# A fused attention-and-experts kernel: hand-written queue orders changed on all five engines, and four turn banks instead of two for the last tile

## The reference

```
q(v)  = (clip(round(v / s + z), 0, 255) - z) * s
x = x + tanh(g_x) * matmul(q1(layernorm(x)), q2(ctx))
y = layernorm(x)
logits = y @ route_w.T                     # the best of 8 experts per row
wh = onehot(argmax) * max(logits) * (y @ A.T)
x = x + tanh(g_f) * (wh @ B.T)
```

## Time and profile before

| what | us |
|---|---|
| median of three executions (lowest, highest) | 364.46 (363.89, 364.64) |
| the profiled execution | 363.53 |
| its span, first to last instruction | 361.7 |
| PE busy | 333.0 (92%) |
| DVE busy | 260.6 (72%) |
| ACT busy | 197.4 (55%) |
| POOL busy | 172.3 (48%) |

### The profile page before, as it was taken

The page is one execution under the profiler, slowest core; times in us unless marked ns, Lnnn a source line. Parts: engine busy times, 40 slices in busy tenths (PEclk is TensorE's granted clock), DMA queues, the critical chain, the costliest instruction groups (busy, mean ns, idle before and its releaser), DMA issues.

```text
span 361.7 us, 5854 instructions
## 1 busy us (share of the span) xinstructions
PE 333.0 (92%) x2237; PEld 186.4 (52%) x2262; DVE 260.6 (72%) x553; ACT 197.4 (55%) x129; POOL 172.3 (48%) x199
## 2 busy tenths in 40 slices
PE   0389999999999999999998999999999999999983
PEld 0244454546756466455464546464464555465751
DVE  3855799898967896958658587945588567585853
ACT  1888489778967262747999270524062413204460
POOL 2559267431265162545999056627064441605281
PEclk9999999999999999999999999999999999999999
DMA  7999999895769998899799996666939890443956
GB/s 301 400 387 404 366 387 380 289 348 173 284 182 212 289 251 291 270 266 294 176 366 157 262 320 121 181 111 177 212 138 158 225 288 31 93 84 59 304 220 232
DMA packets 93906, 87.63 MB, mean 242 GB/s; under 512 B 71844, under 2 KB 72868, under 8 KB 89764
## 3 DMA queue, kind: packets, MB, share of 16 engines
q1 hardware_dynamic: 93856, 87.11, 79.5%
q10 hardware_dynamic: 12, 0.00, 0.0%
HBM read 52.49 MB, written 16.78 MB: 191 GB/s over the span
## 4 chain that ended last, share of the span: by engine, by line
PE 77%; DVE 8%; DMA 7%; issue 2%; ACT 2%; POOL 2%; ACTq 0%; SPq 0%; DVEq 0%
PE main L1575 46%; DMA xs<-in_x 4%; PE hp L1613 4%; PE hp L1617 4%; PE hp L1614 4%; PE outp L1575 4%; PE outp L1658 4%; PE outp L1660 3%; PE outp L1659 3%; DVE bn L971 3%; PE turn L1609 2%; DMA prow<-in_g_ffn 2%; DMA out<-xs 1%; ACT x L753 1%; PE turn L1503 1%
## 5 line engine op out<-in xcount | busy, mean ns | idle before, releaser
L1575 PE MATMUL main<-q,qa 128*128 128x512 bf16 x841 | 194.6, 380 | 5.0 <-POOL q L593 2.3
L1575 PEld LDWEIGHTS main<-q,qa 128*128 128x128 bf16 x864 | 83.2, 98 | 101.2 <-issue 2.7
L586 POOL TENSOR_TENSOR yn<-y,yn 128x2048 f16<-128x2048 f32 x13 | 53.0, 4077 | 31.7 <-ACT y L788 31.7
L735 ACT ACTIVATE c<-stage,zpc,inv 128x2048 int8<-128x2048 f32 x24 | 49.9, 2086 | 7.7 <-DMA stage<-in_ctx 4.0
L593 POOL CAST q<-c 128x2048 bf16<-128x2048 int8 x24 | 45.1, 1893 | 15.3 <-ACT c L735 14.8
L782 ACT ACTIVATE yn<-xs,sc 128x2048 f16<-128x2048 f32 x11 | 23.0, 2093 | 53.4 <-POOL sc L579 49.6
L1104 DVE SCALAR_TENSOR_TENSOR xs<-main,cc,xs 128x512 f32<-128x512 f32 x45 | 33.3, 740 | 21.7 <-PE main L1575 21.5
L574 POOL TENSOR_SCALAR ve<-mv 128x1 f32<-128x1 f32 x16 | 3.1, 191 | 84.8 <-DVE mv L1137 81.8
L1184 DVE SCALAR_TENSOR_TENSOR xs<-outp,tsc,xs 128x512 f32<-128x512 f32 x44 | 31.2, 735 | 13.6 <-PE outp L1660 13.5
L971 DVE BATCH_NORM_STATS2 bn<-xs 128x6 f32<-128x512 f32 x52 | 32.1, 680 | 10.6 <-DMA xs<-in_x 10.6
L753 ACT ACTIVATE x<-xs,sc 128x2048 int8<-128x2048 f32 x12 | 25.0, 2087 | 24.5 <-POOL sc L566 24.4
(11 more groups left out here) (132 smaller groups left out, 435.2 us busy)
## 6 DMA issues: line engine op xcount, KB each, us to landing
stage<-in_ctx SPq DMA_DIRECT2D x24, 1024.0 KB, 7.9
xs<-in_x SPq DMA_DIRECT2D x13, 1024.0 KB, 6.5
out<-xs SPq DMA_DIRECT2D x12, 1024.0 KB, 5.0
yT<-in_ctx SPq DMA_DIRECT2D x4, 1024.0 KB, 9.2
y<-in_ctx SPq DMA_DIRECT2D x4, 1024.0 KB, 10.1
c<-in_x SPq DMA_DIRECT2D x3, 1024.0 KB, 7.4
out<-c SPq DMA_DIRECT2D x3, 1024.0 KB, 7.3
c<-in_L_ffn_A SPq DMA_DIRECT2D x1, 1024.0 KB, 11.5
```

Of the source, the lines that this page charges most:

```text
L586: pool.tensor_tensor(yn[:, 1, :], y[:, :], yn[:, 0, :], ALU.subtract).then_inc(s_ylo_made, 1)
L735: act.activation(c8_of(piece), place(piece), ACT.Identity, bias=zpc[:, 1:2], scale=inv[:, 1:2])\
L1575: last = pe.matmul(bank_of(n)[:, :], q1T(t)[:, k, :], q2[:, nb, k, :], start=(k == 0), stop=(k == KC - 1))
```

## The change

All lists of calls are reordered, with no call added or removed; nearly every tile is touched. One mechanism is new: groups 2 and 3 of tile 15's second transposition go to the two main banks, `y_bank(15, 2)` = `mainp[1]` and `y_bank(15, 3)` = `mainp[0]`, and wait until the last two half blocks have been read.

```diff
+        def y_bank(t, g):
+
+            return mainp[3 - g] if t == T - 1 and g >= 2 else turn[g % 2]
...
+                elif t < T - 1:
+                    pe.wait_ge(s_y_split, 4 * YT.index(t) + g - 1)
                 else:
-                    pe.wait_ge(s_y_split, 4 * YT.index(t) + g - 1)
+
+                    pe.wait_ge(s_half_added, 1)
+                    pe.wait_ge(s_main_added, UNIT[T - 1, NB - 1] + 1)
```

```diff
 (PE, tiles 0 to 3, last block)
-            turn_b(0)
-            turn_b(1)
             column_sums(0, [3])
             main(0, 3, 0)
             main(0, 3, 1)
+            turn_b(0)
+            turn_b(1)
+            main(0, 3, 2)
             turn_b(2)
-            turn_b(3)
-            main(0, 3, 2)
             main(0, 3, 3)
             column_sums(1, [3])
             main(1, 3, 0)
+            turn_b(3)
...
+            turn_q1(4, 0)
+            turn_q1(4, 1)
             column_sums(2, [3])
             main(2, 3, 0)
             main(2, 3, 1)
             main(2, 3, 2)
-            spread_scales()
-            turn_q1(4, 0)
-            turn_q1(4, 1)
+            main(2, 3, 3)
             turn_y(0, 0)
             turn_y(0, 1)
-            main(2, 3, 3)
-            h_group(0, 0)
+            spread_scales()
```

```diff
 (DVE, same place)
             add_main(0, 3)
             stats2_sum(0)
             unit_terms(1, 3)
+            take_b(3)
+            scale_b()
+            take_q1T(4, 0)
+            take_q1T(4, 1)
             add_main(1, 3)
 (SP, batch change)
             load_ctx(30)
+            load_ctx(31)
             load_x(9)
-            load_ctx(31)
 (DVE, tile 8)
             add_experts(5, 0)
+            add_experts(5, 1)
             stats1(9)
             tile_terms(8)
             add_main(8, 0)
             add_main(8, 1)
-            add_experts(5, 1)
```

```diff
 (PE, the end)
+            expert_product(12, 1)
             main(15, 2, 2)
+            main_half(0, 0)
             main(15, 2, 3)
-            main_half(0, 0)
+            expert_product(12, 2)
             main_half(0, 1)
             main_half(1, 0)
             main_half(1, 1)
-            expert_product(12, 1)
-            expert_product(12, 2)
             h_rows_high(14)
             expert_product(12, 3)
             turn_wh(13)
             h_rows_low(14)
+            turn_y(15, 0)
+            turn_y(15, 1)
+            turn_y(15, 2)
             expert_product(13, 0)
             expert_product(13, 1)
-            turn_y(15, 0)
+            turn_y(15, 3)
...
             expert_product(14, 0)
             expert_product(14, 1)
+            expert_product(14, 2)
             h_group(15, 2)
             h_group(15, 3)
-            expert_product(14, 2)
             expert_product(14, 3)
 (DVE, the end)
             add_main(14, 2)
+            gate(13)
             add_main(14, 3)
-            gate(13)
 (ACT, the end)
+            high_part(15, 0)
             scale_part(13, 0)
             scale_part(13, 1)
-            high_part(15, 0)
             high_part(15, 1)
+            high_part(15, 2)
+            take_wh(14)
             scale_part(13, 2)
             scale_part(13, 3)
-            take_wh(14)
-            high_part(15, 2)
+            scale_part(14, 0)
             high_part(15, 3)
-            scale_part(14, 0)
```

More of the change, by code:

```diff
@@ L446, in _ @@
             load_ctx(12)
+            load_x(4)
             load_ctx(13)
@@ L471, in _ @@
             store(2)
+            load_ctx(25)
             load_ctx(26)
@@ L497, in _ @@
             flip_q1(10)
+            store(6)
             flip_high(9)
-            store(6)
+            load_x(13)
             flip_low(9)
             flip_q1(11)
-            store(7)
             flip_high(10)
@@ L505, in _ @@
             flip_q1(12)
-            load_x(13)
+            store(7)
+            store(8)
             load_x(14)
+            load_x(15)
             flip_high(11)
@@ L510, in _ @@
             flip_q1(13)
-            store(8)
+            store(9)
             flip_high(12)
-            load_x(15)
             flip_low(12)
             flip_q1(14)
-            store(9)
+            store(10)
             flip_high(13)
@@ L940, in _ @@
             norm_full(12)
+            affine_x(14)
             affine_x(15)
@@ L1240, in _ @@
             widen_x(2)
+            stats1(3)
             take_q1T(2, 0)
             take_q1T(2, 1)
+            scale_a()
             see_q1(2)
+            widen_x(3)
             unit_terms(0, 0)
@@ L1292, in _ @@
             unit_terms(2, 3)
-            take_scales()
-            take_q1T(4, 0)
-            take_q1T(4, 1)
             low_part(0, 0)
             low_part(0, 1)
+            take_scales()
+            low_b()
             add_main(2, 3)
-            low_b()
             stats2_sum(2)
             unit_terms(3, 3)
+            add_main(3, 3)
             low_part(0, 2)
@@ L1319, in _ @@
             add_main(4, 1)
+            add_main(4, 2)
             gate(2)
-            take_q1T(5, 0)
-            add_main(4, 2)
+            add_experts(1, 0)
+            add_experts(1, 1)
             add_main(4, 3)
@@ L1423, in _ @@
             gate(10)
+            stats1(14)
             add_experts(9, 0)
@@ L1681, in _ @@
             main(1, 0, 3)
+            turn_q1(3, 0)
             column_sums(2, [0])
             main(2, 0, 3)
+            turn_q1(3, 1)
             main(1, 1, 0)
+            main(0, 1, 0)
+            main(3, 0, 0)
+            main(3, 0, 1)
             main(1, 1, 1)
@@ L1697, in _ @@
             column_sums(2, [1])
+            main(3, 0, 2)
             main(2, 1, 3)
-            turn_q1(3, 0)
-            turn_q1(3, 1)
-            turn_a(0)
-            main(3, 0, 0)
             main(3, 1, 0)
@@ L1717, in _ @@
             main(0, 2, 2)
-            turn_a(3)
             main(0, 2, 3)
@@ L1768, in _ @@
             h_group(0, 1)
-            turn_y(1, 0)
-            turn_y(1, 1)
-            h_group(0, 2)
-            h_group(0, 3)
             column_sums(4, range(NB))
@@ L1867, in _ @@
             main(7, 0, 0)
-            h_rows_low(5)
+            main(7, 0, 1)
             main(7, 1, 0)
             main(7, 1, 1)
-            main(7, 0, 1)
+            turn_q1(7, 1)
+            h_rows_low(5)
             main(7, 0, 2)
+            main(7, 1, 2)
             main(7, 0, 3)
-            main(7, 1, 2)
             main(7, 1, 3)
             main(7, 2, 0)
+            main(7, 3, 0)
+            main(7, 2, 1)
             expert_product(4, 2)
-            main(7, 2, 1)
-            main(7, 3, 0)
+            expert_product(4, 3)
             main(7, 3, 1)
-            expert_product(4, 3)
-            turn_wh(5)
             main(7, 2, 2)
```

401 lines of the change are left out of this document (195 added, 206 removed).

## The result

| | before | after |
|---|---|---|
| median of 19 executions each, us (lowest, highest) | 363.99 (363.08, 365.10) | 365.89 (364.21, 371.13) |
| the profiled execution, us | 363.53 | 364.21 |
| its span, us | 361.7 | 362.4 |

The changed kernel is slower: the ratio of the times is 1.0055, with a 95% interval of 1.0039 to 1.0071, or 2.0 us of 364. The forecast was 1.5 us faster. The new order also scatters more: its executions lie 5.5 us apart, those of before 2 us; the one of 371.13 us, over 1.5% above the fastest, is left out of this and of the ratio. The profiled execution of after is the fastest of the 19, so the trace shows at least part of the loss, not all of it.

The account below looks back on a forecast made before the run. PE, busy almost without break from 54 to 350 us, was taken as the bound, so only closing gaps could win. Terms +0.2 - 1.4 - 0.9 - 0.2 + 0.8 = -1.5 us gave a 363.0 us median, range 361.2 to 365.8.

Parts of the forecast that it names:

- Start: Up to block 2 of tile 0: reordered early loads cost +0.2 us, bounds -1.7 and +2.5.
- The walk: Start, followed load by load: `main(0, 0, 0)` near 21.5 us at half rate, block 2 of tile 0 at 54.7.
- R1: Rival, slower: sparse start becomes the bound, PE waits at 35.4 us for late ctx4 and ctx5; 365.3 alone, chance 0.24.
- End of the ramp: 54 to 94 us: PE's waits for `take_b`, `add_main(0, 3)` and `take_q1T(4)` go; -1.4 us, bounds -1.8 and +1.
- both thin covers: End of ramp: additions ready at 82.8 and 88.8 us, wanted by PE at 83.8 and 89.6, about 1 us spare each.
- Batch change: Gap ahead of 193.87 us: x9's chain comes earlier and is wanted later; -0.9 us, bounds -1.4 and +0.6.
- a third to all of a piece: Batch change: share of ctx31's 2.7 us ahead of x9, leaving 0 to 1.8 us of gap; 0.5 taken.
- The rest of the middle: 94 to 336 us outside the batch change: small gaps close, -0.2 us, bounds -0.5 and +2.
- End: From 336 us: `expert_product(14, 2)` ahead of the last two groups, plus small waits; +0.8 us, bounds +0.4 and +1.7.
- the tail of 11.86 us: Behind the last `h_group`: gate, `take_wh`, last experts and quarter stores, taken as call for call the same.
- R2: Rival, no difference: ctx31 ahead of x9 keeps the gap at 193, or thin covers are used up; 363.9 to 364.6, chance 0.24.
- R1 with a second gap: Late loads at the start plus one new 1.4 us gap in the thin covers: 366 us, left out of the range.

Follow-up runs that it names:

- changed_again: The changed kernel run again with nothing altered (the repeat): 366.28 us, ratio 1.0052 to the kernel before.
- x9_first: The changed kernel with `load_x(9)` put back ahead of `load_ctx(31)` on SP: 364.83 us, ratio 1.0020 to the kernel before.
- new_middle: The kernel before with the changed lists from about 100 us to about 322 us: 365.90 us, ratio 1.0061.
- tile7_back: The changed kernel with `turn_q1(7, 1)`, `h_rows_low(5)` and two expert products of tile 5 at their old PE places: 366.06 us, ratio 1.0064 to before.
- x7_first: The changed kernel with `load_x(7)` ahead of `load_ctx(26)` on SP: 367.74 us, ratio 1.0115 to the kernel before.
- two_pieces_apart: The changed kernel with `load_ctx(25)` ahead of `store(1)` on SP and `affine_ctx(23)` ahead of `take_wh(1)` on ACT: 366.99 us, ratio 1.0085 to before.
- end_from_14: The kernel before with the changed lists from tile 14 on and the four banks: 364.92 us, ratio 1.0035.
- changed_old_end: The changed kernel with the lists of before and two banks from tile 14 on: 364.88 us, ratio 1.0039 to the kernel before.

## Why the prediction was wrong, point by point

**Start, forecast +0.2, measured +0.62.** The walk was right to 0.4 us. `main(0, 0, 0)` started at 21.97 us (21.5 forecast), eight matmuls took 3.57 us at half rate, and block 2 of tile 0 started at 55.02 with `turn_a(3)` done (54 to 55.5 forecast). The loads from x2 to ctx5 landed within 1 us of the walk (x2 at 10.5, x3 at 21.1, ctx4 at 29.0, ctx5 at 32.1). One reading of before was wrong, without an effect on this: x2 landed at 16.0 us, not at 18.2, since the 15.2 us of the earlier trace rows belong to the load of x4, issued at 29.32. No load stopped PE between 26 and 54 us, so R1 did not happen. The first lines of PE:

```profile
19.26 1.87 PE L1507 MATMUL turn<-idb,q 128*128 128x128 bf16 x16 [3.09 <-DVE qa L1025]
21.97 3.57 PE L1579 MATMUL main<-q,qa 128*128 128x512 bf16 x8 [0.84 <-DVE qa L1025]
25.34 1.26 PE L1507 MATMUL turn<-idb,q 128*128 128x128 bf16 x16
26.43 1.89 PE L1579 MATMUL main<-q,qa 128*128 128x512 bf16 x8
```

Eight matmuls take 3.57 us at 21.97 and 1.89 us at 26.43: the engine changed from 1.2 to 2.4 GHz between 25 and 26 us, where before it had done so near 20.5. PE had stood idle for 3.09 us ahead of 19.26, which it had not before.

**End of the ramp, forecast -1.4, measured -1.91.** Right in kind, a third larger than forecast, and both thin covers held: PE has no wait from 55 to 94 us.

**Batch change, forecast -0.9, measured -0.24 in the profile and +0.16 in the repeat.** The mechanism was right (the chain is earlier and wanted later, and with x9 ahead of ctx31 the gap closes as the sum said). The step that failed is the size that I took for ctx31: I let half a microsecond of gap stand for a third to all of a piece, and took a value near the good end with no row for it. The whole piece, 2.7 us, comes first. x9_first shows what this term cost: 1.1 us in the median, 1.3 by the ratios.

**The rest of the middle, forecast -0.2, measured +1.67** (94 to 190 and 200 to 336 us: -0.12, +1.58, +0.21), and more in the repeat, whose gap at 150 us is 1.54 and not 0.59. By the profile this is the step that turned the sign. I wrote that stores, loads and flips of SP are shifted "by a place or two" and priced that at small gaps, without walking a single one. Two pieces now stand right ahead of x7, which is issued 3.8 us earlier than before (138.03 against 141.85) and takes 3.6 us longer. So it lands only 0.2 us earlier than before, where PE comes out of the ramp over 1 us earlier. It lands 1.3 us later than before in the repeat, and 1.2 us later in new_middle, which has the old ramp. Meanwhile `stats1(7)` on DVE holds up `add_experts(3, 1)`. Two expert products of tile 5 stand right behind `turn_wh(5)`, so the 0.6 us through ACT is uncovered. `main(7, ...)` waits for an addition behind `gate(5)`, since `h_rows_low(5)` moved later. The upper bound of +2 covered it, so the time was a question of the value taken and not of the bounds. These gaps are not a price for each: with ctx31 still ahead of x9, closing two of them (tile7_back) gained nothing, and closing the one at 150 us (x7_first, two_pieces_apart) opened another of 2.2 or 1.6 us elsewhere. That the middle as a whole costs about 2 us is shown by new_middle. How that divides between these gaps and the batch change is not.

**End, forecast +0.8, measured +0.70 in the profile and +1.3 us in end_from_14's median.** Ahead of the gate +0.74: the wait of `h_rows_low(14)` was 0.6 of the 0 to 0.7, and 0.39 us at 348.3 is `expert_product(14, 2)` waiting for `scale_part` to empty its bank, which I had not seen. Behind it +0.64 - 0.68. The size is near, the reason was half wrong: I took the tail of 11.86 us for fixed, so that the 0.65 us "cannot be hidden". The tail is set by `store(14)` and the DMA engines when PE runs at full rate, and by PE when it doesn't.

**Sum.** By the profile's steps: +0.62 - 1.91 - 0.24 + 1.67 + 0.70 = +0.84 us against my -1.5, and the first transposition gave 0.16 back. Of the 2.3 us between, 1.9 are the rest of the middle and 0.7 the batch change. The median is 1.7 us worse than this profile. The profiled repeat, itself 0.9 us above its median, has 0.95 us more at 150 us, 0.4 more at the batch change and 0.7 more in the tail. Of the rivals, R2's mechanism (ctx31 ahead of x9) is true, but its time is not the result; no rival had a late load other than those of the start and x9. (R1 with a second gap is 366.7 us by its own terms, 365.3 and 1.4, and not 366; it did not happen.) The measured 365.9 lies just above the range, whose upper end took in one bad term at a time and not the two that came.

**What stays open.** The medians of the changed kernel's parts do not add up cleanly: the middle alone costs 2.2 us, the end alone 1.3, start and ramp 0 to +0.3 (with their own gap), and all three together 2.0. The scatter of 5.5 us is explained in part at most.

## What to carry to other kernels

When an order written out by hand is changed everywhere, each read that is moved must be walked, not only those at known gaps: it lands behind what was issued ahead of it in the same queue, and one 1 MB piece more is 2.7 us here. Landings must be walked in the order of issue, not each from its own issue. A gain ahead of a chain that is timed by transfers (store, load, statistics) is for the most part waited for again at that chain, so count gains from the last such chain on, and attack the chain first: two calls exchanged in one queue gave 1.1 us, and with the orders around it 1.5. Three orders are coupled through one buffer (ACT frees it, SP loads it, everything behind the load waits), so a call put back on one engine alone can cost 15 us.

## What the runs showed of the hardware that I had not expected

The granted clock can fall again in the tail, where PE waits for the last gate. Timeline of PE in end_from_14 and then in after, the same experts of tile 15:

```profile
354.67 0.61 PE L1666 MATMUL outp<-BT,whT 128*128 128x512 f16 x1 [0.48 <-ACT whT L797]
355.07 0.63 PE L1667 MATMUL outp<-BT,whT 128*128 128x512 f16 x1
```
```profile
354.88 0.39 PE L1666 MATMUL outp<-BT,whT 128*128 128x512 f16 x1 [0.48 <-ACT whT L797]
355.11 0.38 PE L1667 MATMUL outp<-BT,whT 128*128 128x512 f16 x1
```

The granted clock from 354 to 358 us is 0.56 to 0.58 in the first and 1.00 in the second, and the starts are 0.43 and 0.22 us apart: the two levels of 1.2 and 2.4 GHz. What PE had done before was the same wait of 2.0 us in both (the gate's, shown in the experiments on the end), and the profiles do not say why the clock fell in one and not in the other. In changed_old_end it fell after a wait of only 1.3 us. From the first `turn_wh(15)` to the last matmul it costs 1.0 to 1.2 us (4.94 in changed_again, 5.12 in end_from_14, 3.93 in before and after). So a profile's own time must be read with its tail, and an order whose tail hangs on the stores hardly feels it (0.1 us or less in changed_old_end).
